# Two loads moved from SyncE to GpSimd, and the gathers released two steps earlier, in the mixture-of-experts part of a two-layer kernel

## The chip, the cores and the metric

The kernel runs on one core of a Trainium2 chip. The metric is the device time of one execution in microseconds (us). An execution of the kernel before took 1237.13 us in the median of three (1232.06, 1237.13, 1239.69).

## What is computed

The reference is a two-layer block over x, 16 x 256 tokens of width 256, in float32: an mLSTM cell and a LoRA feed-forward layer, then cross attention, then a mixture of experts. The change lies in the last part:

```python
def _L1_ffn_ref(x, router_w, router_b, w1, b1, w2, b2, sw1, sb1, sw2, sb2):
    xf = x.reshape(-1, D)                                   # 4096 tokens
    sh = gelu(jnp.einsum('nd,sdh->snh', xf, sw1) + sb1[:, None, :])
    shared_out = (jnp.einsum('snh,shd->nd', sh, sw2) + sb2.sum(0)) / S     # 2 shared experts
    gates = xf @ router_w + router_b
    topv, topi = jax.lax.top_k(gates, TOP_K)                # 2 of 8 experts
    probs = jax.nn.softmax(topv, axis=-1)
    comb = jnp.einsum('nke,nk->ne', jax.nn.one_hot(topi, E, dtype=xf.dtype), probs)
    h = gelu(jnp.einsum('nd,edh->enh', xf, w1) + b1[:, None, :])
    y = jnp.einsum('enh,ehd->end', h, w2) + b2[:, None, :]
    moe_out = jnp.einsum('ne,end->nd', comb, y)
    return (shared_out + moe_out).reshape(B, L, D)
...
x = x + jnp.tanh(g_ffn[1]) * _L1_ffn_ref(_layernorm(x, axis=-1), ...)
```

## The kernel before

Each engine runs one instruction stream that is written out by hand; the streams meet in semaphores. A stream works strictly in order. x stays in SBUF (`x_all`) from start to end. Matrix products are done in three passes over a high and a low part of each operand (`three_passes`, lines 32 to 34), so most tiles exist as `_hi` and `_lo`.

The mixture of experts has three stages, and on each engine they follow each other without a barrier.

**Routing** (`moe_route`), 16 chunks of 256 tokens. Tokens are normalised, transposed, kept in DRAM (`zt_kept`), put through the router and through the first shared expert. GpSimd scatters the normalised rows into the DRAM tensor `z_rows`, sorted by expert (`scatter`, line 2220; semaphore `scattered`), two indirect DMAs for each 128 tokens. Pad rows are cleared by SyncE (`padded`). VectorE writes the table `M.tiles_at`: for each of 39 tiles of 256 sorted rows, its expert and its first row (`tables_done`). At the end of routing SyncE reads the table and loads the weights of the first two tiles (`e_raw`, line 2195) and the rows of the first two tiles (`z_in`, lines 2196 to 2201).

**Experts** (`moe_experts`), 39 tiles: transpose `z_in`, multiply by `w1` of the tile's expert, GELU, multiply by `w2`, store to `y_rows`. The rows of tiles 2 to 38 are loaded by GpSimd (`load`, lines 2750 to 2755), their weights by SyncE (lines 2714 to 2720). The first transposes stand in TensorE's stream inside routing (`turn_pe`, line 2701): after the hidden products of chunk 15, and ahead of the output products of chunks 14 and 15. They wait for `M.z_in_loaded`. At the stage's start SyncE loads the weights of the second shared expert (`s1_raw`, `s2_raw`, 512 KB each, lines 2736 and 2737) and the first kept chunk (`first_kept`, line 2724). These buffers lie where rows that the scatters read have lain, so SyncE first waits. Before, it waits for `z_in` (line 2735), which implies the scatters.

**Combining** (`moe_combine`), 16 chunks: the second shared expert, 4 hidden blocks (KF = 4) for a chunk, each with two GELUs on ScalarE. GpSimd fetches the experts' results of the chunk's tokens with indirect DMAs, four for a chunk (2 blocks of 128 tokens, 2 experts each), into one of 4 slots (RR = 4; the slots are parts of `w2_lo`, and are called `d_w_lo` in the rows). VectorE adds them to x times their probability (`weigh`, line 2973) and counts `weighed`; it then adds the shared expert's output (line 2980), and SyncE stores the chunk.

What releases a gather before, for chunk n and block t:

```python
            after(pool, weighed, T * TOP * (n - RR + 1))
            for t in range(T):
                after(pool, gelu_hi, KF * n + (KF // T) * t - 1)
```

So the GELU count must have reached 4n - 1 for the first block and 4n + 1 for the second.

Of the kernel before, what the change touches and what calls it, by code (L numbers as in the profile page):

```python
# [21 lines left out]
P = 128  # L22
# [80 lines left out]
class Mlstm:  # L103

    B, S, D, H = 16, 256, 256, 8
# [1273 lines left out]
class RoutedRows:  # L1379


    TILES = 4
# [666 lines left out]
def moe_route(nc, S, M, ctx, sem_of, x_all, tanh_g, ident, half_neg, routed, w1_in, router_b, b1_in, w2_in, b2_in, z_rows, zt_kept):  # L2049
# [96 lines left out]
    def on_sync(sync):  # L2146
# [46 lines left out]
        for u in range(2):  # L2193
            e = sync.value_load(M.tiles_at[:, 0, u:u + 1], min_val=0, max_val=E - 1)
            sync.dma_start(M.e_raw[u][:], w1_in[bass.ds(e, 1)].rearrange("e p f -> p (e f)")).then_inc(M.e_loaded[u], 16)
        at = [sync.value_load(M.tiles_at[:, 1, u:u + 1], min_val=0, max_val=(E + 1) * S.ROWS - TOK) for u in range(2)]
        sync.wait_ge(padded, 16 * (E + 1))
        for half in range(2):
            sync.wait_ge(scattered[half], 16 * TILES * TOP // 2)
        for u in range(2):  # L2200
            sync.dma_start(M.z_in[u][:], z_rows[bass.ds(at[u], TOK), :].rearrange("(t p) d -> p t d", p=P)).then_inc(M.z_in_loaded[u], 16)
        for u in range(ZR):
            sync.wait_ge(zt_stored[u], 32 * ((CHUNKS - 1 - u) // ZR + 1))

    def on_gpsimd(pool):
# [34 lines left out]
        for h in range(CHUNKS):  # L2240
            if PT * (h + 3) < TILES:
                rstds(h + 3)
            if h >= 2 and PT * (h - 2) < TILES:
                for i in range(PT * (h - 2), PT * (h - 1)):
                    scatter(i)

    def on_scalar(act, turn_experts):
        def turn(r):
# [390 lines left out]
def moe_experts(nc, S, M, ctx, sem_of, route, ident, passed, w1_in, w2_in, z_rows, y_rows, zt_kept):  # L2639
# [72 lines left out]
    def on_sync(sync):  # L2712
        def load_w(i, u):
            if prepared(i):
                return
            if isinstance(i, int) and i < 2 * AHEAD:
                sync.wait_ge(route.split_lo, E)
            after(sync, w_lo_done, i - 3)
            e = sync.value_load(M.tiles_at[:, 0, bass.ds(i, 1)], min_val=0, max_val=E - 1)
            sync.dma_start(w_raw[u][:], w1_in[bass.ds(e, 1)].rearrange("e p f -> p (e f)")).then_inc(w_loaded[u], 16)  # L2720

        def load_kept(n):
            after(sync, kept_loaded[n % 2], 16 * (n // 2))
            sync.dma_start(kept_at[n].bitcast(F32), zt_kept[n].rearrange("p k t -> p (k t)")).then_inc(kept_loaded[n % 2], 16)

        def store(i, u):
            if isinstance(i, int) and i == LAST_TILE - 1:
                sync.wait_ge(hid_done, KF * LAST_TILE)
                for n in (1, 2):
                    load_kept(n)  # L2730
            sync.wait_ge(y_copied, i + 1)
            sync.dma_start(y_rows[bass.ds(i * TOK, TOK), :].rearrange("(t p) d -> p t d", p=P), ys[u][:]).then_inc(stored[u], 16)

        for u in range(2):
            sync.wait_ge(M.z_in_loaded[u], 16)
        sync.dma_start(s1_raw[:], w1_in[S.NE - 1, :, 0:KD * FF].rearrange("p (c f) -> p c f", c=KD)).then_inc(last_loaded, 16)
        sync.dma_start(s2_raw[:], w2_in[S.NE - 1]).then_inc(last_loaded, 16)
        load_kept(0)
        pipeline(sync, S.PAIR_TILES, ORDER, {"load_w": load_w, "second": store})
# [139 lines left out]
def moe_combine(nc, S, M, sem_of, route, experts, x_all, tanh_g, zt_kept, y_rows, out):  # L2879
# [44 lines left out]
    def on_gpsimd(pool):  # L2924
        for u in range(2):
            pool.wait_ge(experts.stored[u], 16 * ((S.PAIR_TILES + 1 - u) // 2))
        for n in range(CHUNKS):
            after(pool, weighed, T * TOP * (n - RR + 1))
            for t in range(T):
                after(pool, gelu_hi, KF * n + (KF // T) * t - 1)  # L2930
                for k in range(TOP):
                    pool.indirect_dma_start(rows[n % RR][:, t * TOP + k, :], None, y_rows,  # L2932
                                            bass.IndirectOffsetOnAxis(ap=M.pos[:, T * n + t, k:k + 1], axis=0)).then_inc(gathered[n % RR], 16)
# [198 lines left out]
```

## Time and profile before

| what | value |
|---|---|
| median of three runs | 1237.13 us |
| the profiled execution | 1237.13 us |
| its span | 1235.5 us |
| outside the span | 1.6 us |
| TensorE matmul busy | 1121.5 us, 91% |
| VectorE busy | 890.0 us, 72% |
| ScalarE busy | 698.8 us, 57% |
| GpSimd busy | 426.4 us, 35% |
| mean granted TensorE clock | 0.947 |

The profile names engines PE (TensorE), DVE (VectorE), ACT (ScalarE), POOL (GpSimd) and SP (SyncE). A "q" behind the name is the engine's sequencer, which issues DMAs and reads registers. Times in a timeline are counted from the start of the span, in us. Matmuls are pipelined and their ends are modelled, so a busy TensorE may still be issuing slower than it could: the counts of matmuls in equal stretches tell more. A few per cent of the matmul records can be missing.

### The profile page before, as it was taken

To read this page: it belongs to the slowest core of one execution; us is meant where nothing else is said; L and a number is where in the kernel's file an instruction comes from. 1 tells how busy PE (TensorE), PEld (TensorE's weight loads), DVE (VectorE), ACT (ScalarE), POOL (GpSimd) and SP (SyncE) were. 2 spreads that over 40 slices of the span, in tenths; PEclk is the share of its full clock that TensorE was granted. 3 is DMA by queue.
4 is the path that set the end of the run, shared out by engine and by line. 5 is a ranking of instruction groups with operands and counts; after the bars stand their busy time and mean duration, and the time that the engine had idled before them with its cause. 6 is when DMAs were issued, how large, how long until landed. Compare 5 with 4: busy or idle time off the path is not lost. (4 is left out here: it accounts for less than half of the span.)

```text
span 1235.5 us, 28090 instructions
## 1 busy us (share of the span) xinstructions
PE 1121.5 (91%) x9256; PEld 947.9 (77%) x9257; DVE 890.0 (72%) x2039; ACT 698.8 (57%) x1580; POOL 426.4 (35%) x557
## 2 busy tenths in 40 slices
PE   5858887999998799999998879879999999998997
PEld 1326665788887577777776569779999999998987
DVE  5839998766676788888888468548766667664665
ACT  1359876565654476676675644236755555554443
POOL 1237885713121111111111015664223323223664
PEclk8979989999998899999999879889999999999999
DMA  9246550100003553554552027747555455544664
GB/s 324 69 172 216 199 199 25 53 0 0 0 0 62 122 131 86 108 111 92 106 113 55 2 100 273 256 167 256 180 162 167 158 168 163 169 138 154 192 201 145
DMA packets 97565, 163.51 MB, mean 132 GB/s; under 512 B 12039, under 2 KB 72219, under 8 KB 95163
## 3 DMA queue, kind: packets, MB, share of 16 engines
q1 hardware_dynamic: 87611, 135.04, 37.4%
q0 software_dynamic: 9104, 26.49, 6.6%
q8 instruction: 56, 0.92, 0.3%
q10 hardware_dynamic: 752, 0.73, 0.2%
q14 instruction: 42, 0.34, 0.1%
HBM read 102.47 MB, written 33.69 MB: 110 GB/s over the span
## 5 line engine op out<-in xcount | busy, mean ns | idle before, releaser
L1677 DVE TENSOR_REDUCE c_mx<-c_s 128x2 f32<-128x512 f32 x256 | 164.4, 686 | 20.7 <-PE c_s L1823 20.4
L1598 ACT ACTIVATE c_probs<-c_t 128x512 f32<-128x512 f32 x256 | 139.0, 597 | 28.8 <-PE c_t L1846 27.9
L2772 ACT ACTIVATE d_g_full<-d_bank,d_e_bias 128x256 f32<-128x256 f32 x156 | 77.6, 497 | 106.3 <-PE d_bank L34 106.3
L32 PE MATMUL d_bank<-de_zt_hi,d_e_hi 128*128 128x256 f32 x312 | 91.2, 292 | 0.1
L34 PE MATMUL d_bank<-d_w_hi,d_g_lo 128*128 x312 | 88.0, 282 | 0.0
L33 PE MATMUL d_bank<-d_w_lo,d_g_hi 128*128 x312 | 88.0, 282 | 0.0
L32 PE MATMUL d_bank<-d_w_hi,d_g_hi 128*128 x312 | 87.8, 281 | 0.0
L34 PE MATMUL d_bank<-de_zt_hi,d_e_lo 128*128 128x256 f32 x312 | 87.7, 281 | 0.0
L33 PE MATMUL d_bank<-de_zt_lo,d_e_hi 128*128 128x256 f32 x312 | 87.7, 281 | 0.0
L2801 DVE TENSOR_TENSOR d_g_lo<-d_g_full,d_g_hi 128x256 fp32r<-128x256 f32 x156 | 67.2, 469 | 25.8 <-ACT d_g_hi L2773 25.6
L2932 POOL DMA_INDIRECT d_w_lo<-d_y_rows,d_pos x64 | 65.4, 1022 | 52.0 <-ACT d_g_hi L2945 19.3
L1531 POOL CAST c_ct_hi<-c_c_raw 128x512 fp32r<-128x512 f32 x15 | 9.2, 612 | 211.7 <-PE c_misc L34 211.7
L2773 ACT ACTIVATE d_g_hi<-d_bank,d_e_bias 128x256 fp32r<-128x256 f32 x156 | 78.3, 502 | 0.0
L32 PE MATMUL d_bank<-d_s_hi,d_g_hi 128*128 128x256 f32 x256 | 75.2, 294 | 2.4 <-DVE d_g_lo L2964 1.3
L34 PE MATMUL d_bank<-d_s_hi,d_g_lo 128*128 128x256 f32 x256 | 74.5, 291 | 2.4 <-issue 2.3
L33 PE MATMUL d_bank<-d_s_lo,d_g_hi 128*128 128x256 f32 x256 | 74.2, 290 | 2.5 <-issue 2.5
L32 PE MATMUL d_bank<-d_w_hi,d_sw_hi 128*128 128x256 f32 x232 | 70.1, 302 | 6.9 <-ACT d_g_hi L2262 3.6
L1846 PEld LDWEIGHTS c_t<-c_qt,c_kt 50*128 50x128 f32 x512 | 39.2, 189 | 47.7 <-ACT c_probs L1598 22.0
L1846 PE MATMUL c_t<-c_qt,c_kt 50*128 50x256 f32 x512 | 65.8, 336 | 9.1 <-ACT c_probs L1598 5.1
L1858 PE MATMUL c_o<-c_probs,c_va 128*32 128x256 f32 x1024 | 71.3, 398 | 1.2 <-ACT c_probs L1598 1.2
L673 ACT ACTIVATE a_decay<-a_mb,a_tok_all 128x256 f32<-128x256 f32 x128 | 65.8, 514 | 10.3 <-POOL a_mb_late L612 7.7
L34 PE MATMUL d_bank<-d_w_hi,d_sw_lo 128*128 128x256 f32 x232 | 68.9, 297 | 2.8 <-issue 2.6
(412 smaller groups left out, 3800.6 us busy)
## 6 DMA issues: line engine op xcount, KB each, us to landing
d_e_raw<-in_w SPq DMA_DIRECT2D x39, 514.0 KB, 3.6
a_mb<-a_maxima SPq DMA_DIRECT2D x16, 1024.0 KB, 7.5
d_w_hi<-d_zt_kept SPq DMA_DIRECT2D x26, 512.0 KB
d_y_rows<-de_ys SPq DMA_DIRECT2D x39, 256.0 KB, 2.1
d_z_in<-d_z_rows POOLq DMA_DIRECT2D x37, 256.0 KB, 4.0
c_kt<-c_k_hi SPq DMA_DIRECT2D x64, 128.0 KB, 3.2
c_qt<-c_q_hi SPq DMA_DIRECT2D x64, 128.0 KB, 3.7
d_zt_kept<-d_w_hi SPq DMA_DIRECT2D x32, 256.0 KB
```

The lines of the kernel that those rows point to most:

```text
L32: tensor.matmul(out, lhs_hi, rhs_hi, start=start, stop=False)
L33: tensor.matmul(out, lhs_hi, rhs_lo, start=False, stop=False)
L34: return tensor.matmul(out, lhs_lo, rhs_hi, start=False, stop=stop)
L673: act.activation(decay[:, h % DR, 0:S], mb[u][:, h, :], ACT.Exp, scale=-1.0, bias=tok_all[:, 0, 0, k:k + 1]).then_inc(decay_done, 1)
L1598: act.activation(probs[h % PR][:], t_ps[k][:], ACT.Exp).then_inc(exp_done, 1)
L1677: dve.tensor_reduce(mx[n % 2][:, :, k, p:p + 1], s_ps[h % SB][:], AX.X, ALU.max).then_inc(max_done, 1)
L1846: mm = pe.matmul(t_ps[k][:, i, :], kt[u][rows, p, i * P:(i + 1) * P], qt[u][rows, p, :], start=True, stop=True)
L1858: mm = pe.matmul(o_ps[OSLOT * i:OSLOT * (i + 1), g % 2, :], va[n % R][:, j, h, :], probs[(n * H + h) % PR][:, j, :], start=(j == 0), stop= ...
L2772: act.activation(g_full[:, m, :], hid[m][:, 0:TOK], ACT.Gelu, bias=bias[u][:, m:m + 1]).then_inc(gelu_full, 1)
L2773: act.activation(g_hi[u][:, m, :], hid[m][:, 0:TOK], ACT.Gelu, bias=bias[u][:, m:m + 1]).then_inc(gelu_hi, 1)
L2801: dve.tensor_tensor(g_lo[u][:, m, :], g_full[:, m, :], g_hi[u][:, m, :], ALU.subtract).then_inc(gelu_lo, 1)
L2932: pool.indirect_dma_start(rows[n % RR][:, t * TOP + k, :], None, y_rows, bass.IndirectOffsetOnAxis(ap=M.pos[:, T * n + t, k:k + 1], axis=0 ...
```

## The change

The loads of `z_in` for the first two tiles move from SyncE to GpSimd, behind the last scatter. SyncE's wait for them, ahead of the shared-weight loads, becomes the wait for the scatters alone. And in the last stage each gather is released two GELU steps earlier: the count must have reached 4n - 3 and 4n - 1, where it was 4n - 1 and 4n + 1.

```diff
@@ on_sync of moe_route @@
         for u in range(2):
             e = sync.value_load(M.tiles_at[:, 0, u:u + 1], min_val=0, max_val=E - 1)
             sync.dma_start(M.e_raw[u][:], w1_in[bass.ds(e, 1)].rearrange("e p f -> p (e f)")).then_inc(M.e_loaded[u], 16)
-        at = [sync.value_load(M.tiles_at[:, 1, u:u + 1], min_val=0, max_val=(E + 1) * S.ROWS - TOK) for u in range(2)]
-        sync.wait_ge(padded, 16 * (E + 1))
-        for half in range(2):
-            sync.wait_ge(scattered[half], 16 * TILES * TOP // 2)
-        for u in range(2):
-            sync.dma_start(M.z_in[u][:], z_rows[bass.ds(at[u], TOK), :].rearrange("(t p) d -> p t d", p=P)).then_inc(M.z_in_loaded[u], 16)
@@ on_gpsimd of moe_route, at its end @@
+        pool.wait_ge(padded, 16 * (E + 1))
+        for half in range(2):
+            pool.wait_ge(scattered[half], 16 * TILES * TOP // 2)
+        pool.wait_ge(tables_done, 1)
+        for u in range(2):
+            row = pool.value_load(M.tiles_at[:, 1, u:u + 1], min_val=0, max_val=(E + 1) * S.ROWS - TOK)
+            pool.dma_start(M.z_in[u][:], z_rows[bass.ds(row, TOK), :].rearrange("(t p) d -> p t d", p=P)).then_inc(M.z_in_loaded[u], 16)
@@ on_sync of moe_experts @@
-        for u in range(2):
-            sync.wait_ge(M.z_in_loaded[u], 16)
+        for half in range(2):
+            sync.wait_ge(route.scattered[half], 16 * S.TILES * S.TOP // 2)
         sync.dma_start(s1_raw[:], w1_in[S.NE - 1, :, 0:KD * FF].rearrange("p (c f) -> p c f", c=KD)).then_inc(last_loaded, 16)
@@ on_gpsimd of moe_combine @@
             for t in range(T):
-                after(pool, gelu_hi, KF * n + (KF // T) * t - 1)
+                after(pool, gelu_hi, KF * (n - 1) + (KF // T) * t + 1)
```

How this moves instructions. On SyncE, at the end of routing, before the change (`d_e_raw` are expert weights, `de_s_raw` the shared weights, `de_first_kept` the kept chunk, `d_y_rows` the store of a tile; "ISA" rows set registers):

```order
L2195 DMA d_e_raw<-in_w 128x1028
L2196 TENSOR_LOAD d_tiles_at
L2196 ISA x2
L2196 TENSOR_LOAD d_tiles_at
L2196 ISA x2
L2201 ISA
L2201 DMA d_z_in<-d_z_rows 128x2x256
L2201 ISA
L2201 DMA d_z_in<-d_z_rows 128x2x256
L2736 DMA de_s_raw<-in_w 128x1024
L2737 DMA de_s_raw<-in_w 128x1024
L2724 DMA de_first_kept<-d_zt_kept 128x1024
```

On SyncE at the same place after it (line numbers behind the edit are one higher):

```order
L2195 DMA d_e_raw<-in_w 128x1028
L2737 DMA de_s_raw<-in_w 128x1024
L2738 DMA de_s_raw<-in_w 128x1024
L2725 DMA de_first_kept<-d_zt_kept 128x1024
L2720 TENSOR_LOAD d_tiles_at
```

Two register loads and two DMAs are gone between the expert weights and the shared weights. On GpSimd, behind the scatters, before the change (`d_z_rows` is the scatter, L2754 and L2755 the load of a tile's rows, here tiles 2 and 3):

```order
L2220 DMA d_z_rows<-dr_z,dr_pos_i 39168x256 x48
L2754 TENSOR_LOAD d_tiles_at
L2754 ISA x2
L2755 ISA
L2755 DMA d_z_in<-d_z_rows 128x2x256
L2754 TENSOR_LOAD d_tiles_at
```

On GpSimd at the same place after it:

```order
L2214 DMA d_z_rows<-dr_z,dr_pos_i 39168x256 x48
L2245 TENSOR_LOAD d_tiles_at
L2245 ISA x2
L2246 ISA
L2246 DMA d_z_in<-d_z_rows 128x2x256
L2245 TENSOR_LOAD d_tiles_at
L2245 ISA x2
L2246 ISA
L2246 DMA d_z_in<-d_z_rows 128x2x256
L2755 TENSOR_LOAD d_tiles_at
```

The two loads stand between the last scatter and the load of tile 2. The gathers of the last stage stand in the same order before and after; only the counts that they wait for differ.

## Rows read from the trace of the kernel before

**Rows 1.** The page, part 1: busy us (share of the span), instructions

```profile
PE 1121.5 (91%) x9256; PEld 947.9 (77%) x9257; DVE 890.0 (72%) x2039; ACT 698.8 (57%) x1580; POOL 426.4 (35%) x557
```

**Rows 2.** Stretches: length, busy us (instructions) by engine, granted clock, DMA share, GB/s

```profile
858.00:882.00 24.00, 23.88 (x200) 23.48 (x199) 17.46 (x37) 20.26 (x44) 3.65 (x5) 1.00 0.63 226
882.00:1122.00 240.00, 240.00 (x2027) 240.00 (x2026) 161.62 (x299) 131.62 (x334) 67.18 (x106) 1.00 0.50 160
...
1134.00:1147.00 13.00, 9.25 (x45) 7.75 (x44) 5.51 (x13) 5.68 (x15) 8.20 (x9) 0.74 0.37 105
1147.00:1160.00 13.00, 13.00 (x112) 13.00 (x111) 8.17 (x19) 6.21 (x16) 8.60 (x9) 1.00 0.71 219
1160.00:1173.00 13.00, 12.03 (x98) 11.53 (x98) 8.46 (x19) 6.30 (x16) 8.38 (x9) 1.00 0.66 203
```

**Rows 3.** Timeline of SyncE's sequencer, 856 to 868: start, us, instruction

```profile
860.77 0.96 SPq L2201 DMA_DIRECT2D d_z_in<-d_z_rows  x2
864.53 0.35 SPq L2736 DMA_DIRECT2D de_s_raw<-in_w  x1
...
867.48 0.34 SPq L2720 DMA_DIRECT2D d_e_raw<-in_w  x1
```

**Rows 4.** By line, L2199, L2201, L2735: ns min/median/max, first and last start

```profile
L2199 SPq EVENT_SEMAPHORE  x1: 28/28/28, 860.6 to 860.6; - x1
...
DMA to landing us min/median/max: 3.0/3.1/3.1
...
L2735 SPq EVENT_SEMAPHORE  x2: 28/28/28, 863.8 to 864.5; - x2
```

**Rows 5.** Timeline of TensorE, 858 to 874: the transposes of tiles 0, 1

```profile
865.75 0.60 PE L2701 MATMUL d_bank<-ident,d_z_in 128*128 128x128 f32 x4
...
872.90 0.60 PE L2701 MATMUL d_bank<-ident,d_z_in 128*128 128x128 f32 x4
```

**Rows 6.** By line: register load L2754 (from 864 to 880), then L2755's landings

```profile
L2754 POOLq TENSOR_LOAD <-d_tiles_at x3: 290/301/507, 866.5 to 877.9; - x3
...
DMA to landing us min/median/max: 3.1/4.0/5.9
```

**Rows 7.** Timeline of GpSimd, 845 to 885; idle before it in brackets

```profile
855.35 0.96 POOL L2220 DMA_INDIRECT d_z_rows<-dr_z,dr_pos_i  x1 [0.30 <-issue]
868.02 0.79 POOL L2755 DMA_DIRECT2D d_z_in<-d_z_rows  x1 [11.71 <-issue]
```

**Rows 8.** DMA issues from 866 to 869: count, KB, us to landing

```profile
d_z_in<-d_z_rows POOLq DMA_DIRECT2D x1, 256.0 KB, 5.8
```

**Rows 9.** Stretches of 2 us at the hand-over, columns as in rows 2

```profile
860.00:862.00 2.00, 2.00 (x19) 2.00 (x19) 0.31 (x1) 0.17 (x2) 0.00 (x0) 1.00 0.93 352
...
864.00:866.00 2.00, 2.00 (x20) 2.00 (x19) 1.40 (x4) 2.00 (x6) 0.00 (x0) 1.00 0.32 51
866.00:868.00 2.00, 2.00 (x20) 2.00 (x19) 2.00 (x5) 2.00 (x7) 0.00 (x0) 1.00 0.90 334
```

**Rows 10.** Timeline of ScalarE at the hand-over: its copy of tile 0

```profile
868.23 0.67 ACT L2687 ACTIVATE de_zt_hi<-d_bank 128x512 fp32r<-128x512 f32 x1
```

**Rows 11.** Waits, 1100 to 1236: us in total, times, longest

```profile
DVE x_all L2973 <- DMA d_w_lo<-d_y_rows,d_pos: 2.9, 1, 2.9
```

**Rows 12.** Timeline of GpSimd in the last stage: gathers

```profile
1125.12 1.23 POOL L2932 DMA_INDIRECT d_w_lo<-d_y_rows,d_pos  x1 [17.78 <-DMA d_y_rows<-de_ys]
...
1142.63 1.01 POOL L2932 DMA_INDIRECT d_w_lo<-d_y_rows,d_pos  x1 [2.45 <-ACT d_g_hi L2945]
...
1223.75 1.05 POOL L2932 DMA_INDIRECT d_w_lo<-d_y_rows,d_pos  x1 [0.30 <-issue]
```

**Rows 13.** Timeline of VectorE at the end: the last chunk's gathered rows

```profile
1229.33 1.79 DVE L2973 SCALAR_TENSOR_TENSOR x_all<-d_w_lo,d_prob,x_all 128x256 f32<-128x256 f32 x4
```

**Rows 14.** Stretches of 1 us where the clock falls and returns, columns as in rows 2

```profile
1139.00:1140.00 1.00, 0.20 (x2) 0.29 (x1) 0.00 (x0) 0.00 (x0) 0.77 (x1) 0.69 0.33 86
...
1146.00:1147.00 1.00, 1.00 (x9) 1.00 (x9) 0.87 (x4) 0.95 (x3) 0.70 (x2) 0.90 0.40 94
```

## Prediction

> **What bounds the kernel now.** I read the page first [rows 1]: TensorE is busy 91% of the span, no other engine comes near. A share says little about a change that touches two short places, so the next view is the table by stretch [rows 2]. It has one line for the hand-over from routing to experts (858 to 882 us), one for the experts (882 to 1122) and several of 13 us inside the last stage. In the first two TensorE is busy 23.88 of 24 and 240.00 of 240 us: whatever makes TensorE wait at the hand-over is added to the end one for one. In the last stage it is not full. 1147 to 1160 holds 112 matmuls, 1160 to 1173 only 98, and 1134 to 1147 only 45, at a mean granted clock of 0.74. These losses are there before the change, and the diff adds or removes no TensorE instruction.
>
> Then the hand-over, in order. SyncE's issues [rows 3] show the two loads of `z_in` from 860.77, and the first shared-weight load only at 864.53. The views by line [rows 4] say why: the wait for the scatters (L2199) ends at 860.6, each `z_in` load lands 3.1 us after its issue, and the wait for these landings (L2735) ends at 863.8 for the first and 864.5 for the second. TensorE [rows 5] transposes tile 0 at 865.75 with no idle time before it, so the first load has about 865.75 - 863.84 = 1.9 us to spare. The second tile is transposed at 872.90: 8.4 us to spare.
>
> **The change, part by part.** (1) SyncE loses two register loads and the two `z_in` loads. It spent no work time that anybody waited for: its next load of expert weights, at 867.48 [rows 3], stands behind a wait for VectorE's eighth low part (`split_lo`), which splits loaded weights and has nothing to do with `z_in`. Gain: 0.
>
> (2) GpSimd gets a wait for the scatters, the pads and the table, and two register loads and two `z_in` loads. What is queued behind the wait on GpSimd is its load of tile 2, which waits for the transposes of tile 0 in any case. All scatters are issued by 856.3 (the last one 855.35 + 0.96) [rows 7] and complete at 860.6, which is SyncE's figure [rows 4], so GpSimd's wait ends there too. What a load then costs on GpSimd is shown by the first one it does already [rows 6]: register load at 866.5 [rows 6], issue at 868.02 [rows 7], that is 1.5 us; the landing comes 4.0 us after the issue in the median of 37 [rows 6], and 5.8 us for this one [rows 8]. So tile 0 is issued at 860.6 + 1.5 = 862.1. It lands at 862.1 + 4.0 = 866.1 by the median and at 862.1 + 5.8 = 867.9 by the nearest one. Lower bound: the fastest of the 37, 3.1 us, gives 865.2, in time. Tile 1 comes after another 0.79 + 1.5 us [rows 7]: issue 864.4, landing about 870, before 872.90. It costs nothing.
>
> (3) SyncE now waits only for the scatters, and issues the two shared-weight loads and `first_kept` (3 x 512 KB) at about 860.7 to 861.6, not from 864.53. Nobody needs them soon, yet they share the DMA engines with `z_in`. How full these are is in the table [rows 9]: 352 GB/s from 860 to 862 with the present traffic, 51 GB/s from 864 to 866, and 334 after it, when the loads that SyncE held back and the next expert weights are in flight. The change fills the gap just when GpSimd's load is in flight, which is the condition of the load that took 5.8 us, and that is why I take 5.8 and not 4.0. TensorE then starts tile 0 at 867.9 and not 865.75: a wait of 2.2 us. Bounds: 0 (a landing in 3.1 us), and at most 5.2 us, if all of SyncE's bytes go ahead of it: 3 x 524 KB / 330 GB/s = 4.8 us on top of the median landing, 862.1 + 4.0 + 4.8 = 870.9.
>
> Two things hang on TensorE's tile 0. ScalarE copies it at 868.23, with no idle before, since it is full of other work [rows 10]; TensorE's transposes would be done 0.6 us after 867.9, at 868.5, so ScalarE loses 0.3 us, not 2.2. In 858 to 882 TensorE idles some 0.1 us by the table; ScalarE falling behind less than TensorE did gives back at most 0.2 us. Net: +2.0 us.
>
> A rule of the Trainium skill speaks to this edit. The row: SyncE's loads of `z_in` landed 3.1 us after issue, GpSimd's 4.0 in the median and 5.8 in traffic [rows 4, 6, 8]. "DMA: Bandwidth & Descriptors", section "Issuing engines are not separate DMA queues", says that DMAs from any issuing engine run on the same 16 engines and interleave, so that a second issuer saves only its sequencer's time. By that rule the edit has nothing to win, and the trace agrees. The same page's "Specifications" gives about 1 us to the first byte from GpSimd and 0.6 from SyncE; with 0.4 us added to 3.1 the tile lands at 862.1 + 3.5 = 865.6, just in time, and the sum would be 0.
>
> (4) The gathers of the last stage are released two GELU steps earlier. Where would TensorE notice? VectorE adds the gathered rows (L2973). In the whole of that stage it waits for them once, 2.9 us [rows 11], before chunk 0. That wait is not touched: gathers start at 1125.12 when the last expert rows are stored, then run back to back, twelve of them, to 1140.2 (the wait of 2.45 before 1142.63 begins there) [rows 12]. Their rate and their start decide, and the thresholds released now were already met when each was issued. The first real shift comes at 1142.63, where GpSimd sat 2.45 us waiting for ScalarE: two gathers now go out at about 1140.5 and 1141.7, and from there GpSimd is two gathers ahead. The thresholds are the same odd numbers, so the rhythm, the DMA bytes and the number of issues stay. The slots have room: a gather of chunk n needs chunk n-4 added, which happened 5 GELU steps before the new release. At the very end VectorE adds the last chunk at 1229.33 without idle before it [rows 13], and the last gather is issued at 1223.75 [rows 12], 5.6 us before its rows are read: early enough. Gain of (4): 0. What hides it is the slack of the gathers. If that is gone somewhere the trace does not show, the bound is the 2.9 us of the one wait; as a loss, the two gathers in the gap at 1140 could lengthen TensorE's bad stretch by the gap they fill, 2.5 us. I take 0.
>
> The sum: the profiled execution took 1237.13 us (span 1235.5 and 1.6 around it), which is also the median of the three runs. 1237.1 + 2.0 = **1239.1 us**.
>
> **Rivals.** *B: `z_in` lands in time.* The transfer is no slower than its median minus a little, and TensorE doesn't notice: 1237.1. For it: 3.1 us was seen. Against: the traffic moved onto it.
>
> *C, faster: the bad stretch shrinks.* From 1134 to 1147 TensorE issued 45 of about 112 matmuls in 13 us; 13 x (1 - 45/112) = 7.8 us are lost, part of it at a granted clock of 0.50 (1.2 GHz) [rows 2, 14]. ScalarE and VectorE have nothing to do then, so no tile holds TensorE up, and slow feeding of its instructions is what is left. If DMA traffic makes that slow, another timing of gathers and of the store of x may remove it: 1239.1 - 7.8 = 1231.3. Against: up to 1140 the gathers are issued at the same moments as now.
>
> *D, slower: one wait, at tile 0, that pulls the clock down.* The 1.5 MB of SyncE drain first, tile 0 lands at 870.9, TensorE stands still 5.2 us. From 1134.6 thin work of about that length was followed by the lower clock from inside 1139 to 1140 until inside 1146 to 1147 [rows 14]; some 6.4 us at half rate cost 3.2 us. Sum 8.4: 1245.5. It decides from the point where the wait passes some 5 us; a wait of 2 us leaves the clock alone, since 1160 to 1173 loses 1.6 us with the clock at 1.00 [rows 2]. Against: the DMA engines interleave queues rather than drain one, or the `z_in` load at 868.02 would have taken longer than 5.8 us beside the loads around it.
>
> *E: the gather edit does not do what it says,* because the issue rate holds GpSimd back. In the first twelve gathers that is so; it changes no time, so it is part of the forecast.
>
> **How the numbers follow.** Forecast 0.60, B 0.15, C 0.11, D 0.12, rest 0.02. The likeliest is 1239.1. The runs of before spread from 1232.1 to 1239.7, so each case blurs by some 3 us: C reaches down to about 1229, D up to 1248. Leaving out a tenth on each side: 1231 to 1246.5. What this measurement can tell from no change is about 1%, 12.4 us. None of the cases gets there by itself: faster by over 1% needs C and a good draw (0.03), slower needs D and a longer bad stretch (0.05), within 1% is 0.92.
>
> **What would show it.** In the changed profile: GpSimd's first `z_in` issue at 862 and its landing 4 to 6 us later; SyncE's shared-weight loads at 860.7; TensorE's first transpose 1 to 3 us later against the last matmul before it, where before there was no gap; the stretch from there to the end of the experts unchanged in length; VectorE's one wait for gathers still near 2.9 us; GpSimd's wait after twelve gathers gone. I am wrong if TensorE shows no gap at the transposes (then B), if the gap is over 4 us, if the 13 us stretch after the first gathers changes by more than 3 us, or if VectorE starts to wait for gathered rows.

## The result, and the profile after

| | before | after |
|---|---|---|
| median (lowest to highest), 20 runs each | 1238.44 us (1232.06 to 1242.91) | 1244.82 us (1242.29 to 1251.54) |
| ratio after/before, 95% interval | | 1.0066 [1.0052, 1.0081] |
| the profiled execution: time, span | 1237.13, 1235.5 us | 1246.31, 1244.7 us |

The change costs 6.4 us (0.66%); the forecast was 1239.1, a cost of 2.0. The measured time lies inside the stated range, but the interval leaves out both "no cost" and "two microseconds". It also shows that the bound of 1% that the prediction set for what can be told from no change was too coarse: with 20 runs a side, 0.15% could be told.

The page shows the same matmuls and about the same work on VectorE and ScalarE, so nothing was added but time:

```profile
PE 1131.0 (91%) x9256; PEld 956.5 (77%) x9257; DVE 890.8 (72%) x2039; ACT 699.2 (56%) x1580; POOL 427.4 (34%) x559
```

The answer to [rows 2], by stretch: length, busy us and instructions of TensorE, its weight loads, VectorE, ScalarE and GpSimd, granted clock, DMA share, GB/s. The later stretches are moved by 5.7 us, as the first gather is.

```profile
858.00:882.00 24.00, 21.08 (x166) 20.88 (x165) 14.93 (x33) 16.36 (x35) 2.95 (x4) 0.93 0.63 215
887.70:1127.70 240.00, 240.00 (x2027) 240.00 (x2026) 161.86 (x298) 131.61 (x334) 67.65 (x106) 1.00 0.49 160
1139.75:1152.75 13.00, 7.70 (x27) 5.42 (x27) 2.14 (x5) 3.60 (x10) 7.54 (x9) 0.64 0.35 101
1152.75:1165.75 13.00, 13.00 (x108) 13.00 (x108) 9.64 (x23) 7.19 (x20) 8.30 (x9) 0.96 0.61 201
1165.75:1178.75 13.00, 10.57 (x74) 10.47 (x74) 7.91 (x19) 4.91 (x13) 7.42 (x8) 0.87 0.61 192
```

Two places changed, and the 240 us between them did not (2027 matmuls in both). At the hand-over 34 matmuls fewer fit into 24 us. In the last stage the bad stretch holds 27 matmuls, not 45, at a mean clock of 0.64, not 0.74, and a second weak one follows (74 matmuls at 0.87, where before had 98 at 1.00).

Four milestones that both traces have put the 9.2 us between the two profiled spans in their places:

| from, to | before | after | difference |
|---|---|---|---|
| start to the issue of the last scatter | 855.35 | 856.94 | +1.6 |
| last scatter to the transposes of tile 0 | 10.40 | 13.58 | +3.2 |
| tile 0 to the first gather (the experts) | 259.37 | 260.35 | +1.0 |
| first gather to the last addition to x | 106.04 | 109.50 | +3.5 |

The first line lies ahead of every edited instruction, and a second profile of the unchanged kernel (`e9_before_third`, below) reaches its `z_in` loads 4.0 us later than the first did. It is spread between executions, and is why the spans differ by more than the medians.

**The hand-over.** First SyncE's sequencer (start, us, instruction), then GpSimd (idle before it in brackets), then the landing times of the two moved loads, answering [rows 3, 7, 8]:

```profile
862.06 0.34 SPq L2737 DMA_DIRECT2D de_s_raw<-in_w  x1
862.44 0.43 SPq L2738 DMA_DIRECT2D de_s_raw<-in_w  x1
862.91 0.43 SPq L2725 DMA_DIRECT2D de_first_kept<-d_zt_kept  x1
```

```profile
856.94 0.96 POOL L2214 DMA_INDIRECT d_z_rows<-dr_z,dr_pos_i  x1 [0.30 <-issue]
863.70 0.79 POOL L2246 DMA_DIRECT2D d_z_in<-d_z_rows  x1 [5.80 <-issue]
864.88 0.74 POOL L2246 DMA_DIRECT2D d_z_in<-d_z_rows  x1 [0.39 <-issue]
...
DMA to landing us min/median/max: 6.3/6.5/6.8
```

SyncE and GpSimd wait for the same scatters. SyncE's 1.5 MB of loads start at 862.06, GpSimd's `z_in` only at 863.70, behind all of them, and lands 6.8 us later. TensorE and ScalarE at that place, answering [rows 5, 10]:

```profile
870.52 1.11 PE L2702 MATMUL d_bank<-ident,d_z_in 128*128 128x128 f32 x4 [2.92 <-DMA d_z_in<-d_z_rows]
```

```profile
871.67 0.60 ACT L2688 ACTIVATE de_zt_hi<-d_bank 128x512 fp32r<-128x512 f32 x1 [1.84 <-PE d_bank L2702]
```

The releaser in brackets is the moved load: a wait of 2.92 us, where before had none. The four transposes then take 1.11 us, not 0.60. Stretches of 2 us say why, answering [rows 9]:

```profile
866.00:868.00 2.00, 1.61 (x14) 1.40 (x13) 1.39 (x3) 2.00 (x5) 0.00 (x0) 1.00 0.94 344
868.00:870.00 2.00, 0.00 (x0) 0.00 (x0) 2.00 (x7) 1.84 (x6) 0.00 (x0) 1.00 0.86 297
870.00:872.00 2.00, 1.48 (x7) 1.48 (x8) 0.57 (x2) 0.33 (x1) 0.00 (x0) 0.61 0.82 267
872.00:874.00 2.00, 2.00 (x12) 2.00 (x11) 0.69 (x1) 1.98 (x3) 0.71 (x1) 0.54 0.67 251
874.00:876.00 2.00, 2.00 (x19) 2.00 (x19) 0.43 (x1) 1.97 (x4) 0.00 (x0) 1.00 0.50 148
```

TensorE stood still for 2.9 us and came back at nearly half the granted clock (1.2 GHz of its 2.4), so that 872 to 874 is full at 12 matmuls instead of 19. The DMA engines are at 0.94 and 0.86 while the tile is awaited; in [rows 9] they had come down to 0.32 before the tile was needed.

**The last stage.** GpSimd's gathers (the first, the 14th, the first after a pause, the last), VectorE's one wait for gathered rows, and its last chunk, answering [rows 11 to 13]:

```profile
1130.87 1.19 POOL L2933 DMA_INDIRECT d_w_lo<-d_y_rows,d_pos  x1 [17.79 <-DMA d_y_rows<-de_ys]
...
1147.67 0.95 POOL L2933 DMA_INDIRECT d_w_lo<-d_y_rows,d_pos  x1 [0.30 <-issue]
1151.94 1.01 POOL L2933 DMA_INDIRECT d_w_lo<-d_y_rows,d_pos  x1 [3.32 <-ACT d_g_hi L2946]
...
1231.45 0.95 POOL L2933 DMA_INDIRECT d_w_lo<-d_y_rows,d_pos  x1 [0.30 <-issue]
```

```profile
DVE x_all L2974 <- DMA d_w_lo<-d_y_rows,d_pos: 2.8, 1, 2.8
```

```profile
1238.55 1.79 DVE L2974 SCALAR_TENSOR_TENSOR x_all<-d_w_lo,d_prob,x_all 128x256 f32<-128x256 f32 x4
```

The edit does what its diff says: 14 gathers go out back to back, not 12, before GpSimd waits. Nobody was waiting for them: VectorE's one wait is 2.8 us (2.9 before), and its last chunk starts without idle time. Yet TensorE is worse off. Three stretches of 5 us, from 8 us after the first gather, first before, then after:

```profile
1133.12:1138.12 5.00, 3.22 (x21) 2.46 (x20) 2.29 (x5) 1.68 (x4) 3.78 (x5) 1.00 0.53 158
1138.12:1143.12 5.00, 3.03 (x10) 2.29 (x11) 0.43 (x1) 1.60 (x4) 2.25 (x3) 0.63 0.27 79
1143.12:1148.12 5.00, 5.00 (x33) 5.00 (x33) 4.33 (x11) 3.37 (x9) 3.78 (x5) 0.69 0.43 125
```

```profile
1138.87:1143.87 5.00, 2.77 (x18) 2.05 (x16) 1.72 (x4) 0.84 (x2) 3.81 (x4) 0.96 0.55 157
1143.87:1148.87 5.00, 2.86 (x7) 1.62 (x7) 0.43 (x1) 0.84 (x2) 3.80 (x4) 0.50 0.36 105
1148.87:1153.87 5.00, 4.06 (x17) 3.75 (x18) 1.83 (x5) 2.60 (x7) 1.63 (x2) 0.51 0.14 39
```

Before, TensorE is full again (33 matmuls) in the third of them; after, it has 17. Its idle time in the stretch is put down to "issue", not to a tile, and VectorE and ScalarE have little to do meanwhile. The rows of the 14th gather and of the pause behind it (1148.62 to 1151.94) stand just where the recovery begins.

### The profile page after: what moved, and what is told of

It is laid out like the page before. It is cut to its first block and busy times, and to the rows that moved or that the text cites. A ratio compares the mean times of both kernels' runs of the same rounds, so it can differ in the third digit from the quotient of the medians.

```text
span 1244.7 us, 28091 instructions
## 1 busy us (share of the span) xinstructions
PE 1131.0 (91%) x9256; PEld 956.5 (77%) x9257; DVE 890.8 (72%) x2039; ACT 699.2 (56%) x1580; POOL 427.4 (34%) x559
## 5 line engine op out<-in xcount | busy, mean ns | idle before, releaser
L34 PE MATMUL d_bank<-de_zt_hi,d_e_lo 128*128 128x256 f32 x312 | 87.8, 281 | 0.0
L32 PE MATMUL d_bank<-d_w_hi,d_g_hi 128*128 x312 | 87.8, 281 | 0.0
L2933 POOL DMA_INDIRECT d_w_lo<-d_y_rows,d_pos x64 | 62.9, 983 | 56.4 <-ACT d_g_hi L2946 19.4
L32 PE MATMUL d_bank<-d_w_hi,d_sw_hi 128*128 128x256 f32 x232 | 71.3, 307 | 5.5 <-issue 4.7
L33 PE MATMUL d_bank<-d_w_hi,d_sw_hi 128*128 128x256 f32 x232 | 70.0, 302 | 4.5 <-issue 4.5
```

The costliest lines, as they stand in the source:

```text
L32: tensor.matmul(out, lhs_hi, rhs_hi, start=start, stop=False)
L33: tensor.matmul(out, lhs_hi, rhs_lo, start=False, stop=False)
L34: return tensor.matmul(out, lhs_lo, rhs_hi, start=False, stop=stop)
```

## The experiments

The runs were timed in four batches, and each is compared with the kernel before of its own batch. The ratio is estimated over the runs of a batch and can differ a little from the ratio of the two medians; a cost in us is this ratio times the median of before, where nothing else is said. **The kernel before itself showed two levels:** in the first two batches it took 1204 us, in the last two 1237 and 1241, as in the result (1238); the second and the third batch were on the same chip, so the level is no property of a chip. It was not something I set, and its cause stays open. The level decides what the gather edit does, so each table names it. "Last stage" is from the first gather to the last addition to x, in the profiled execution.

Where the levels part can be read from two profiles of the unchanged kernel, the one before the change (span 1235.5 us) and `e6_before_again` (1202.2 us):

| from, to | level 1240 | level 1204 |
|---|---|---|
| start to the first scatter | 755.0 | 755.5 |
| first scatter to the last | 100.4 | 86.8 |
| last scatter to the first gather | 269.8 | 266.4 |
| first gather to the last addition to x | 106.0 | 89.1 |

So 30.5 of the 33.3 us lie in the two stretches in which GpSimd issues indirect DMAs. At the lower level these go out back to back (the last 48 scatters, then all 64 gathers), at the upper one with pauses.

**Level 1204.** The edits: `e1_loads_only` is after with the line of the gathers undone; `e2_gathers_only` is before with that line alone:

```diff
-                after(pool, gelu_hi, KF * n + (KF // T) * t - 1)
+                after(pool, gelu_hi, KF * (n - 1) + (KF // T) * t + 1)
```

`e3_pool_loads_sync_held` is e1, but SyncE again waits for `z_in` before its shared-weight loads. `e4_sync_loads_not_held` is before without that wait:

```diff
-        for u in range(2):
-            sync.wait_ge(M.z_in_loaded[u], 16)
```

> The z_in loads on GpSimd and SyncE's earlier shared-weight loads, without the gather edit. The change cost 6.4 us in the medians. Theory H (the hand-over is the cause: TensorE waits 2.9 us for tile 0 and then runs some 4 us at the lower clock): most of it is here, 3.5 to 5 us over the kernel before, and TensorE's gap at the first transposes is 2 to 4 us. Rival G (the gathers are the cause; 3.5 us of the 9.2 us of the profiled span came in the last stage): this one is at most 3 us over.

> The gather edit alone, loads as before. Theory H: within 1.5 us of the kernel before, VectorE's wait for gathers still one of 2.9 us, no gap at the first transposes. Rival G: 3 us or more over it, all of it between the first gather and the end, with more time at the lower clock there.

> As the loads-only kernel, but SyncE again waits for both z_in landings before the shared weights, so that these do not share the DMA engines with z_in. Theory T (traffic delays z_in): the landing falls from 6.8 us to 3.5 to 4.2 us after issue, TensorE's gap falls to 0.5 us or less, and the time is within 1.5 us of the kernel before. Rival S (the slower issue on GpSimd is enough: 1.5 us to get the load out, and a longer landing whatever is beside it): a gap of 1.5 us or more stays, and the time is within 1 us of the loads-only kernel.

> The kernel before with one wait of SyncE's taken out: z_in is loaded by SyncE as before, the shared weights follow at once instead of after its landing (the scatters have been waited for already). Theory T in its strong form (traffic alone suffices): z_in lands later than 3.1 us, by 1 to 3 us, and TensorE shows a gap. Rival S: SyncE's own loads are taken in order, z_in is first in its queue and lands in 3.1 to 3.5 us; no gap, time as before within 1 us.

| run | median us | before | ratio [95%] | `z_in` issue, after the end of the last scatter's issue | landing us | TensorE waits at tile 0 |
|---|---|---|---|---|---|---|
| e1 | 1210.13 | 1204.38 | 1.0047 [1.0029, 1.0064] | GpSimd, 3.1 | 6.3 | 8.1 |
| e2 | 1203.25 | 1204.38 | 0.9988 [0.9973, 1.0004] | SyncE, 1.6 | 2.8 | 3.1 |
| e3 | 1207.25 | 1204.38 | 1.0026 [1.0006, 1.0047] | GpSimd, 3.1 | 3.2 | 7.5 |
| e4 | 1204.79 | 1204.38 | 0.9992 [0.9974, 1.0010] | SyncE, 1.6 | 2.8 | 3.0 |

At this level GpSimd's scatters run back to back until the end of routing, and TensorE waits for tile 0 in the kernel before too; every microsecond at the hand-over is then on the path. The rows of e1, then those of e3: the last scatter, the load, the landings.

```profile
849.40 1.45 POOL L2214 DMA_INDIRECT d_z_rows<-dr_z,dr_pos_i  x1 [0.31 <-issue]
853.99 0.79 POOL L2246 DMA_DIRECT2D d_z_in<-d_z_rows  x1 [3.14 <-issue]
...
DMA to landing us min/median/max: 6.2/6.3/6.4
```

```profile
841.13 0.96 POOL L2214 DMA_INDIRECT d_z_rows<-dr_z,dr_pos_i  x1 [0.31 <-issue]
845.24 0.79 POOL L2246 DMA_DIRECT2D d_z_in<-d_z_rows  x1 [3.14 <-issue]
...
DMA to landing us min/median/max: 3.1/3.2/3.4
```

The load is issued 3.14 us after the last scatter's issue ends in both. What differs is the landing: 3.2 us when SyncE's loads are held back, 6.3 when they run ahead. That is 3.1 us from traffic. And e4, SyncE's timeline and the landings of its own loads:

```profile
848.64 0.96 SPq L2201 DMA_DIRECT2D d_z_in<-d_z_rows  x2
849.84 0.35 SPq L2734 DMA_DIRECT2D de_s_raw<-in_w  x1
...
DMA to landing us min/median/max: 2.8/2.8/2.9
```

The same three loads released just as early, 0.2 us behind the second `z_in` load, do no harm when `z_in` stands before them in SyncE's own order: 2.8 us. So the traffic costs only because the move to GpSimd made `z_in` the last to be issued. TensorE's waits also hold how early TensorE itself arrives, which differs between executions (8.1 in e1, 11.4 in e5 below, for the same hand-over); the time from the end of the last scatter's issue to tile 0 differs less. It is 4.39 us in e2 and 4.47 in e4, 6.29 in e3, and 9.39 in e1: 1.9 us from e2 to e3 (1.5 for the later issue, 0.4 for GpSimd's longer landing) and 3.1 for the traffic, 5.0 in all, beside a median cost of 5.7 (0.47%). e3 by itself costs 0.26%, 3.1 us. That lies between its two theories (at most 1.5 us, or as much as e1): both causes have a part.

e2 costs nothing here, and the trace of it says why it could not: GpSimd's 64 gathers stand back to back with no pause over 1 us in it, nor in the profile of the kernel before at this level. The thresholds are always met first, and the edit is idle. Stretches of 13 us from the first gather of the kernel before at this level (`e6_before_again`):

```profile
1108.75:1121.75 13.00, 13.00 (x112) 13.00 (x111) 7.69 (x21) 7.83 (x22) 9.95 (x11) 1.00 0.56 185
1121.75:1134.75 13.00, 13.00 (x112) 13.00 (x111) 7.82 (x20) 7.71 (x22) 9.96 (x11) 1.00 0.71 222
```

TensorE is full with 112 matmuls at full clock, there is no bad stretch, and the last stage takes 89.1 us, not 106.

**Level 1204, the second batch.** To see the hand-over by another way, `e7_before_turn_later` gives TensorE some routing work to do before it turns to tile 0, and `e8_after_turn_later` does it to after:

```diff
             hidden_late(h, h % 2)
+            output(h - 1, (h - 1) % 2)
             if h == CHUNKS - 1:
                 turn_experts(pe)
-            output(h - 1, (h - 1) % 2)
```

`e5_after_again` and `e6_before_again` are the two kernels unchanged.

> The changed kernel beside the single parts. Theory H (hand-over alone): the same distance as the loads-only kernel had, 4.5 to 6.5 us over the kernel before, with the last stage as long as before within 1 us where TensorE is fed evenly. Rival G (gathers add 3 us in the last stage): 8 us or more over.

> The kernel before once more, for its profile beside the next three. On a chip where TensorE is fed without slow stretches (last stage 88 to 90 us from first gather to last add, as in the four runs before) it waits some 3 us for tile 0 already; on one with slow stretches (last stage near 106 us) it has about 2 us to spare.

> The kernel before, but TensorE does the output products of chunk 14 (24 matmuls, 2.9 us) before the transposes of tile 0. Theory H: where TensorE waited 3 us for tile 0, the wait shrinks to under 0.5 us and the clock stays up: 2.5 to 4.5 us faster than before. Where it did not wait: within 1 us. Rival (the hand-over is bound by the chain behind tile 0: copy, low part, first GELUs): the wait moves to the next product, and nothing is gained.

> The changed kernel with the same reordering. Theory H: the 2.9 us of products come off the wait, so it is 2.5 to 3.5 us faster than the changed kernel, but still over the kernel before, whose wait is 5 us shorter. Rival: no faster than the changed kernel.

| run | median us | before | ratio [95%] | landing us | TensorE waits at tile 0 | last stage |
|---|---|---|---|---|---|---|
| e5 | 1210.86 | 1204.06 | 1.0070 [1.0043, 1.0096] | 7.0 | 11.4 | 87.8 |
| e6 (one run) | 1203.82 | 1204.06 | | 2.7 | 5.6 | 89.1 |
| e7 | 1200.89 | 1204.06 | 0.9983 [0.9967, 0.9999] | | 0.3 | 88.7 |
| e8 | 1207.19 | 1204.06 | 1.0023 [1.0005, 1.0040] | 7.2 | 9.1 | 88.6 |

The change costs 0.70% at this level too, and all of it ahead of the last stage. e7 leaves 0.3 us of the wait and is the one version that beats before here, by 0.17%, just outside the noise (one of thirteen ratios, so no more than a hint); the clock at its tile 0 stays at 1.00. Its tile 0 to the first gather takes 257.8 us, against 261.2 in e6, but 2.9 us of that is only the output products of chunk 14, which now stand ahead of tile 0. The fair measure, the last scatter to the first gather, is 263.7 against 266.4: 2.7 us gained in these profiles. e8 still waits 9.1 us, so the cover is too short for the later load.

**Level 1237.** The third batch repeats before, the gather edit, and e7 with the gather edit. It ran on the same chip as the second and met the other level:

> The kernel before, third profile. It tells on which kind of chip this call runs: last stage near 106 us (fed in slow stretches) or near 89 us (fed evenly). Only on the first kind can the next run say whether the gathers had a part in the 3.5 us that the last stage grew in the changed kernel's profile there.

> The gather edit alone, second time. Theory H: no difference on either kind of chip (within 1.5 us). Rival G: 2 to 4 us over the kernel before on a chip with slow stretches, nothing on an evenly fed one.

> The version with the later transposes, with the gather edit added. Theory H: what the later transposes gained (2 to 3 us under the kernel before) and nothing more. Rival: the earlier gathers, which take some of VectorE's waits for gathered rows away, add a gain of their own of 1 us or more.

**Level 1241.** In the fourth batch the gathers are released four GELU steps earlier than before (`e12_gathers_4_earlier`), two steps later (`e13_gathers_2_later`), and e1 and e7 are repeated (`e14_loads_only_again`, `e15_turn_later_again`). The edits of e12 and e13:

```diff
-                after(pool, gelu_hi, KF * n + (KF // T) * t - 1)
+                after(pool, gelu_hi, KF * n + (KF // T) * t - 5)
```

```diff
-                after(pool, gelu_hi, KF * n + (KF // T) * t - 1)
+                after(pool, gelu_hi, KF * n + (KF // T) * t + 1)
```

> The kernel before with the gathers released 4 GELU steps earlier instead of 2. Theory F (TensorE's instructions arrive slowly while gathers are issued back to back, and it recovers about 2 us after they pause): where TensorE is fed in slow stretches, at least 14 to 16 gathers go out before the first pause, the slow stretch ends 20 us or more after the first gather (17.5 and 20.0 in the two profiles of the kernel before), and the time is 4 to 9 us over the kernel before. Rival N (the two-step edit met an unlucky phase, no dose): 0 to 5 us over, no more than two steps cost. Where TensorE is fed evenly (kernel before at 1204): no difference, by both.

> The kernel before with the gathers released 2 GELU steps later. Theory F: with slow stretches, the first pause comes after some 10 gathers, the slow stretch ends 2 to 3 us sooner than in the kernel before, and the time is 2 to 4 us under it. Rival N: equal or slower, since VectorE gets its rows later. Fed evenly: VectorE waits more for gathered rows, the time is the same or up to 3 us over.

> The loads alone, second time. With slow stretches: TensorE comes to tile 0 later against the scatters, so its wait is 2 to 4 us and not 8, and the cost 2 to 4 us; together with the 5 us of the gathers about the 6.4 us measured, or somewhat more. Fed evenly: 5.7 us again.

> The later transposes alone, second time. With slow stretches there is no wait for tile 0 in the kernel before, so nothing to gain: within 1 us, or up to 2 us over if ScalarE's copy of tile 0 comes late. Fed evenly: 2 us under the kernel before, as the first time.

In this table all times are us after the first gather. The first bad stretch goes from where starts of TensorE's matmuls come to lie over 0.3 us apart to where they are close again; in brackets, what these gaps add up to. The pause is GpSimd's first of over 0.8 us, and where a second follows after only two more gathers, both are given.

| run | gathers released | median us | before | ratio [95%] | gathers ahead of the pause, and its start | first bad stretch (lost) | last stage |
|---|---|---|---|---|---|---|---|
| before | old | | | | 12, 15.1 | 9.5 to 17.5 (6.2) | 106.0 |
| e9 (one run) | old | 1240.65 | 1236.97 | | 12, 15.2; 14, 18.4 | 9.7 to 20.0 (7.4) | 105.6 |
| e14 | old | 1247.05 | 1241.47 | 1.0038 [1.0019, 1.0057] | 10, 12.5 | 8.2 to 14.8 (5.0) | 106.8 |
| e15 | old | 1242.99 | 1241.47 | 1.0023 [1.0005, 1.0040] | 10, 12.5; 12, 16.4 | 8.3 to 17.8 (5.6) | 104.8 |
| after | 2 earlier | 1244.82 | 1238.44 | 1.0066 [1.0052, 1.0081] | 14, 17.8 | 8.7 to 19.9 (9.1) | 109.5 |
| e10 | 2 earlier | 1242.46 | 1236.97 | 1.0041 [1.0022, 1.0060] | 16, 20.6 | 9.8 to 22.8 (11.1) | 109.9 |
| e11 | 2 earlier | 1243.99 | 1236.97 | 1.0059 [1.0041, 1.0077] | 14, 17.7 | 9.0 to 20.2 (8.9) | 108.5 |
| e12 | 4 earlier | 1246.54 | 1241.47 | 1.0040 [1.0021, 1.0059] | 16, 20.5 | 8.1 to 22.9 (11.6) | 109.5 |
| e13 | 2 later | 1244.86 | 1241.47 | 1.0026 [1.0010, 1.0043] | 8, 10.0 | 8.2 to 11.6 (2.3) | 111.1 |

The loads by themselves (e14) cost 0.38%, 4.7 us of 1241. Its hand-over is that of after: TensorE, then stretches of 2 us.

```profile
874.52 0.93 PE L2702 MATMUL d_bank<-ident,d_z_in 128*128 128x128 f32 x4 [2.73 <-DMA d_z_in<-d_z_rows]
```

```profile
872.00:874.00 2.00, 0.00 (x0) 0.00 (x0) 2.00 (x6) 2.00 (x7) 0.00 (x0) 1.00 0.85 344
874.00:876.00 2.00, 1.48 (x8) 1.48 (x9) 1.06 (x4) 0.84 (x3) 0.00 (x0) 0.69 0.83 245
876.00:878.00 2.00, 2.00 (x11) 2.00 (x11) 0.69 (x1) 1.98 (x3) 0.71 (x1) 0.50 0.73 265
```

The gathers by themselves (e10) cost 0.41%, 5.1 us of 1237. 0.38 and 0.41 make 0.79, inside the interval of both together (0.52 to 0.81). At this level no profile with the gather edit alone has a wait at tile 0. The first bad stretch has one pattern over all nine profiles: it begins 8 to 10 us after the first gather and ends 1.4 to 2.5 us after the gathers pause (after the second pause, where two are given), wherever the thresholds put that pause, from 10.0 us (e13) to 20.6 (e10). The two ends of the series, three stretches of 5 us from 8 us after the first gather in e10 (16 gathers), and two in e13 (8 gathers):

```profile
1133.72:1138.72 5.00, 3.08 (x22) 2.43 (x20) 2.32 (x5) 1.68 (x4) 3.78 (x5) 1.00 0.55 158
1138.72:1143.72 5.00, 3.01 (x6) 1.65 (x6) 0.00 (x0) 0.83 (x2) 3.65 (x4) 0.53 0.37 105
1143.72:1148.72 5.00, 1.58 (x6) 1.67 (x7) 0.43 (x1) 0.23 (x2) 1.96 (x2) 0.50 0.28 80
```

```profile
1137.91:1142.91 5.00, 3.17 (x23) 2.77 (x22) 1.93 (x4) 1.35 (x4) 1.96 (x3) 1.00 0.42 131
1142.91:1147.91 5.00, 5.00 (x45) 5.00 (x44) 4.07 (x10) 4.71 (x13) 4.08 (x4) 1.00 0.27 80
```

In e13 the clock does not fall and TensorE is full (45 matmuls) 13 us after the first gather, where e10 has 6. The first stretch moved as theory F of e12 and e13 expected, and e12's cost of 5.0 us fits it; but e13 was also expected to come out 2 to 4 us under before. It does not: it pays later. Two further rows of e13, 26 to 52 us after the first gather, where before ran 99 and 96 matmuls:

```profile
1155.91:1168.91 13.00, 10.37 (x74) 9.29 (x73) 7.82 (x18) 5.79 (x17) 8.03 (x8) 0.91 0.58 179
1168.91:1181.91 13.00, 13.00 (x95) 13.00 (x95) 8.06 (x18) 5.06 (x14) 7.77 (x8) 0.83 0.59 193
```

So the total does not follow the first stretch: four steps earlier costs 0.40%, two earlier 0.41%, two later 0.26%. The old distance is the best of the four tried, and no version found beats before at this level. That includes e15: from the last scatter to the first gather it takes 270.1 us, as before (269.8) and e9 (270.5). TensorE did not wait for tile 0 there, so the reordering had nothing to gain, and its median is 0.23% above before.

**The later stretches follow the same pattern.** Call gathers with no pause of over 0.8 us between them a run of gathers, and gaps between TensorE's matmuls that add up to 0.6 us or more a stall. Leaving out the first run, the nine profiles at this level hold:

| gathers in the run | runs | with a stall that begins in it or within 1 us behind it |
|---|---|---|
| 2 | 12 | 1 |
| 4 | 25 | 3 |
| 6 | 22 | 10 |
| 8 | 26 | 26 |

No later run has more than 8. The stalls at the runs of 8 lose 0.7 to 4.0 us. In before they are the 1.2 to 1.6 us that TensorE loses about every 13 us: 8 gathers take 10.4 us and the pause behind them 2.5. The eight profiles at the level of 1204 us have one run of 64 gathers each and no stall, so a long run is not enough by itself. Over the whole last stage the stalls lose 13.4 to 14.8 us in the four profiles with the old distance, and 14.7 to 17.6 in the five with another. Each of these five, and e14, also has a later fall of the clock to 0.50, beside a stall that lost 2.2 to 4.0 us; before, e9 and e15 have none until TensorE's work ends.

## Why the prediction was wrong

**(1) SyncE loses its loads: 0.** Right. SyncE's own next loads of expert weights moved without anybody waiting for them.

**(2) GpSimd issues tile 0 1.5 us after the scatters complete.** Right: forecast 862.1 with completion at 860.6; with the 1.6 us by which all of routing was later in this execution that is 863.7, and the row says 863.70. e1 and e3 put it 1.5 us later than SyncE's (3.1 against 1.6 us after the last scatter's issue). The second load followed after 1.2 us, not the 2.3 of the forecast; it cost nothing either way.

**(3) The traffic of the released loads.** The mechanism was right, the size was not. The term was a landing of 5.8 us; it measured 6.8 for this load, 6.3 to 7.2 over the runs. e3 against e1 shows that 3.1 us of it is SyncE's traffic, e4 that the same traffic is harmless in SyncE's own order. The wait is thus 2.9 us, not 2.2. ScalarE, forecast to lose 0.3 us, sat idle for 1.84. The estimate of all 1.5 MB ahead of it (8.8 us) was too long.

**The step that failed here is the clock:** "a wait of 2 us leaves the clock alone", with the point at "some 5 us". A wait of 2.9 us (after), 2.7 (e14) or 3.1 (e2) is followed by between 3 and 4 us at half clock (0.50; the rows of 2 us that hold its start or end show 0.54 to 0.69). I had read [rows 14] as thin work of 5 us and more, and taken the shortest case that I saw for the shortest that there is. The nearest row was a bound from above only, and the range should have held the lower clock at any wait over 2 us. It costs about 1 us by the milestones (tile 0 to the first gather, +1.0), and the hand-over as a whole measured +4.2 in the profile and +4.7 in e14, against "Net: +2.0".

**(4) "Gain of (4): 0."** This step failed, and it is the larger part: 5.1 us by e10, 3.5 by the profiles. What I looked at was who waits for a gather, and there the answer stands: VectorE's wait is unchanged, and so is the end. What I priced at nothing is what gathers do to others while they run. The prediction named the right mechanism as its bound of loss, "the two gathers in the gap at 1140 could lengthen TensorE's bad stretch by the gap they fill, 2.5 us", and took 0 between 2.9 and -2.5 with no row nearer to 0 than to the loss. The profiles give 2.9 us more lost in that stretch (6.2 to 9.1), a little over the bound, and more in a later one, which it did not look for (39 to 43 us after the first gather: 2.9 us lost in after and then the half clock; none of the later stalls of before lost over 1.6).

**The rivals.** *B* (in time) and *C* (the bad stretch shrinks) did not happen. *D*'s 1245.5 is within 1 us of the result, but by half for another reason: its wait of 5.2 us was 2.9, and the rest of the cost is the gathers. Its lower clock was also read a little short: the two rows of [rows 14] span 6.8 us at half rate, not 6.4. *E* holds at the level of 1204 us, where the gather edit releases nothing earlier (e2).

**What is shown and what is argued.** Shown by taking parts away: that the later issue and the traffic make the hand-over's cost; that the gather edit alone costs 0.4% at one level and nothing at the other. Shown as a pattern over nine profiles, in which edits moved the pause but nothing took the gathers' effect away: that the first bad stretch lasts as long as gathers run without a pause. In the later stretches a stall mostly begins before its run ends, and a stalled TensorE also holds back the GELUs that release gathers; there the rows do not separate which ends which.

Not shown is what holds TensorE up. Its gaps name no tile, and VectorE and ScalarE are idle too, which leaves its supply of instructions as a candidate. The Trainium skill, "Runtime: NRT & Kernel Launch", section "Instruction fetch mechanics", says that each engine's sequencer streams its program in 16 KB blocks over a DMA queue of its own, and that crossing from block to block is mostly hidden. The pages of all runs list queues of that kind; q8 (56 packets, 0.92 MB, so 16 KB each) moves one packet for every 102 to 154 of TensorE's matmuls in the last stage. Its packet times speak against it as the cause. In all nine profiles one packet starts 6.3 to 6.7 us after the first gather and takes 1.0 to 1.1 us, ahead of the first bad stretch, and the next starts 28 to 37 us after the first gather. TensorE is back at full pace long before that one (45 matmuls in 5 us in e13), so no late packet of this queue ended the stretch, and the trace agrees with the page that the blocks are hidden. The DMA queues with packets in the first bad stretch of before (1134.6 to 1142.6) are the gathers' and the stores':

```profile
q0 software_dynamic: 288, 0.79, 33.2%
q1 hardware_dynamic: 272, 0.26, 11.3%
```

The amount of DMA traffic is no explanation either. Five us from 8 us after the first gather, at the lower level (e6), have the same DMA share as before's first row of 5 us above (0.54 and 0.53), and 44 matmuls where before has 21:

```profile
1116.75:1121.75 5.00, 5.00 (x44) 5.00 (x43) 3.19 (x9) 2.32 (x8) 3.78 (x5) 1.00 0.54 159
```

**Open:** what sets the kernel's level (1204 or 1240 us), what stops TensorE while some eight gathers in a row go out at the upper one, and why the stalls of the last stage add up to more under either shift of the gathers.

## What to carry to other kernels

Before a load is moved to another issuing engine, look at what the old engine does next: a short, urgent load was safe because it stood first in its own engine's order, and the move gave that place to 1.5 MB that nobody needed. A DMA that is released earlier than anybody needs is not free because nobody waits for it; ask what runs beside it, and price the loss you can name instead of taking 0. And repeat the kernel before beside every batch of runs: here it differed by 3% between batches, and the same one-line edit was free at one level and cost 0.4% at the other.

## What the hardware did that I had not expected

- An idle time of TensorE of 2.7 to 3.1 us was enough for it to run at half its clock (0.50) for between 3 and 4 us afterwards (after, e14, e2).
- The same unchanged kernel took 1204 us in two batches and 1237 to 1241 in two others, on the same chip in two of them, with the same instructions. 30.5 of 33.3 us of it lie where GpSimd issues indirect DMAs: 86.8 against 100.4 us for the scatters, 89.1 against 106.0 for the last stage.
- At the upper level each of the 26 later runs of 8 gathers had a stall of TensorE of 0.7 to 4.0 us towards its end, of the 25 runs of 4 only three; at the lower level 64 gathers in a row had none.
- The cost of a 256 KB load depends on what is issued ahead of it and not on what is released right behind: 2.8 us with 1.5 MB right behind it in SyncE's order (e4), 3.2 from GpSimd with that traffic held back (e3), 6.3 from GpSimd with 1.5 MB issued ahead of it by SyncE (e1). The Trainium skill, "DMA: Bandwidth & Descriptors", section "Issuing engines are not separate DMA queues", says that DMAs from all issuing engines interleave on the same DMA engines; that agrees with e1, while e4 shows that the order of issue still matters.
